# A gated cross-attention and quantised feed-forward block on one core: loads, sums and transposes begin at other places

## What is computed

```python
# x (8, 224, 1024), ctx (8, 750, 1024); Wq, Wk, Wv 1024 x 1024; w1, w2 (2816, 1024), w3 (1024, 2816)
def xattn(x, context):                       # 32 heads of 32
    q = rms(x @ Wq.T); k = rms(context @ Wk.T); v = context @ Wv.T    # rms per head of q and k
    return softmax(q k^T / sqrt(32)) @ v
def ffn(x):                                  # quantise: round(w / mean|w|), clipped to -1..1
    x1 = x @ quantise(w1).T; x2 = x @ quantise(w2).T
    return (sigmoid(x1) * x2) @ quantise(w3).T
x = x + tanh(g_xattn) * xattn(layernorm(x), ctx)
x = x + tanh(g_ffn) * ffn(layernorm(x))
```

## Time and profile before

| | us |
|---|---|
| median of three runs (2461.03 to 2464.95) | 2463.22 |
| the profiled execution, its own time | 2459.92 |
| its span, first to last instruction | 2458.1 |
| PE busy | 2380.9 (97%) |
| DVE busy | 1437.7 (58%) |
| ACT busy | 1351.5 (55%) |
| POOL busy | 856.5 (35%) |
| mean granted clock of TensorE | 0.985 |

### The profile page before, as it was taken

One profiled execution on the slowest core, in us unless ns is written; L12 is line 12 of the kernel. 1 busy time (PEld: TensorE's weight loads), 2 busy tenths in 40 slices (PEclk: granted clock), 3 DMA queues, 4 the chain that ended last, 5 costly groups with the idle time before them and its releaser, 6 DMA issues.

```text
span 2458.1 us, 48877 instructions
## 1 busy us (share of the span) xinstructions
PE 2380.9 (97%) x18386; PEld 1413.2 (57%) x18386; DVE 1437.7 (58%) x2529; ACT 1351.5 (55%) x2886; POOL 856.5 (35%) x857
## 2 busy tenths in 40 slices
PE   7988899999999999999999999878999999999999
PEld 5875466666666666666666666554555555544444
DVE  5656677777776777777767767655444444410000
ACT  5765687787787787887877877752111111110000
POOL 4664245554554645554545546421000000000000
PEclk9998999999999999999999999889999999999999
DMA  6775443343434443433434333444333232344351
GB/s 242 241 242 180 125 102 111 97 119 101 122 93 118 105 107 106 116 116 86 129 102 122 93 93 94 118 122 149 110 95 113 92 114 90 92 137 121 123 163 51
DMA packets 248971, 298.10 MB, mean 121 GB/s; under 512 B 110496, under 2 KB 205216, under 8 KB 248224
## 3 DMA queue, kind: packets, MB, share of 16 engines
q1 hardware_dynamic: 248736, 294.98, 41.3%
HBM read 196.22 MB, written 49.55 MB: 100 GB/s over the span
## 4 chain that ended last, share of the span: by engine, by line
POOL 32%; PE 32%; issue 31%; DMA 2%; DVE 2%; ACT 1%; POOLq 1%; SPq 0%; DVEq 0%; ACTq 0%
PE ps L1435 20%; POOL krs L699 13%; PE ps L1563 11%; POOL oinv L717 4%; POOL qrs L661 3%; POOL kms L694 3%; POOL osum L715 2%; POOL ca L729 2%; POOL osum L722 2%; POOL cn L743 1%; POOL oinv L719 1%; POOL qms L658 1%; DMA hid<-hidden 1%; POOLq L60 1%; PE ps L1420 0%
## 5 line engine op out<-in xcount | busy, mean ns | idle before, releaser
L1467 PE MATMUL ps<-wk,cpair 128*128 128x512 f16 x4608 | 1120.9, 380 | 4.1 <-DVE cpair L1070 3.5
L1267 DVE TENSOR_TENSOR plo<-pf,phi 125x448 f16<-125x448 f32 x768 | 504.6, 658 | 236.1 <-ACT phi L935 229.8
L1467 PEld LDWEIGHTS ps<-wk,cpair 128*128 128x128 f16 x4608 | 400.3, 97 | 379.6 <-issue 6.8
L944 ACT ACTIVATE pf<-ps 125x448 f32<-125x448 f32 x768 | 417.8, 544 | 270.6 <-PE ps L1487 258.6
L1435 PE MATMUL ps<-xnTh,w12q 128*128 128x512 f16 (+1 forms) x1408 | 478.4, 353 | 2.1 <-issue 2.1
L1435 PE MATMUL ps<-xnTl,w12q 128*128 128x512 f16 (+1 forms) x1408 | 478.1, 353 | 0.0
L935 ACT ACTIVATE phi<-pf 125x448 f16<-125x448 f32 x768 | 444.3, 578 | 8.5
L699 POOL TENSOR_TENSOR krs<-kms,mhalf 125x8 f32<-125x8 f32 x192 | 330.0, 1719 | 15.0
L1487 PEld LDWEIGHTS ps<-qT,kst 128*125 128x125 f16 x1536 | 210.1, 138 | 154.2 <-DMA kst<-kpair 7.2
L694 POOL TENSOR_TENSOR kms<-kss,keps 125x8 f32<-125x8 f32 x192 | 69.6, 362 | 625.7 <-DVE kss L1222 625.7
L1511 PE MATMUL ps<-val,phi 125*128 125x65 f16 x3072 | 280.1, 192 | 2.6 <-DVE plo L1267 2.6
(11 more groups left out here) (115 smaller groups left out, 2663.3 us busy)
## 6 DMA issues: line engine op xcount, KB each, us to landing
gbuf<-in_wffn SPq DMA_DIRECT2D x66, 512.0 KB, 4.8
wraw<-in_wffn SPq DMA_DIRECT2D x66, 512.0 KB, 5.7
kst<-kpair SPq DMA_DIRECT2D x128, 250.0 KB, 4.6
cstream<-in_ctx SPq DMA_DIRECT2D x48, 500.0 KB, 4.5
craw<-in_ctx SPq DMA_DIRECT2D x48, 500.0 KB, 6.0
hid<-hidden SPq DMA_DIRECT2D x7, 2816.0 KB, 12.7
hidden<-hh SPq DMA_DIRECT2D x66, 256.0 KB, 2.1
kst<-kpair SPq DMA_DIRECT2D x128, 125.0 KB, 2.5
```

Of the source, the lines that this page charges most:

```text
L944: act.activation(pf[0:KW, e % 6, :], bank(3 + e % 3)[0:KW, 0:2 * S], ACT.Exp, bias=LN128, scale=SCALE).then_inc(p_ready, 1)
L1267: dve.tensor_tensor(plo[0:KW, e % 6, :, :], pf[0:KW, e % 6, :].rearrange("p (t n) -> p t n", t=2), phi[0:KW, e % 6, :, :], ALU.subtract).t ...
L1467: mm = pe.matmul(bank(pt)[:, :], cpair[:, n % RING, a, kc, :], wkp[g][:, w, kc, :], start=(kc == 0 and m == 0), stop=(kc == KC - 1 and m = ...
```

## The change

It does the following, and nothing is computed otherwise:

- Wq is loaded as 16 pieces of 128x512, first the 8 of the left columns, then the 8 of the right; ACT and DVE split them in this order, with `x_norm2(1, 1)` of DVE between the two groups of 8; PE waits piece by piece in both halves of tile 0.
- SP issues the load of x tile n in step n - 3 of phase A rather than n - 2 (tiles 2 and 3 both in step 0).
- `w_squares` of phase A come two at a time, in steps (3, 0), (3, 1), (9, 0), (9, 1).
- The first context tile is split one half-step earlier: ACT after `qnat` of h = 26, DVE at the head of h = 27.
- The 66 absolute sums begin at step 15 of unit 0; steps 11 of units 4 and 5 take one each. SP issues the loads of a unit's sums inside that unit.
- The load of the key/value weights of group 3 moves from unit 0 to unit 1, behind `stack_k`; their squares, sum and splits come later in unit 1, and the power on POOL one tile later.
- The first three `stage` loads are issued in unit 31, and `stage` lies where the dead weights of group 0 were.
- In the tail the transposes use banks 2, 1, 0 in turn, and each waits for the copy three half-tiles back. All 32 matmuls of block 0 come after the tail, and wait for all 28 copies. `thresholds` runs at step 8 instead of 10.

```diff
@@ -127,7 +127,7 @@
         wqraw_scope = ExitStack()
-        wqraw = sb(wqraw_scope, "wqraw", [P, 4, D], F32)
+        wqraw = sb(wqraw_scope, "wqraw", [P, KC, 512], F32)
@@ -182,9 +182,9 @@
         pc = ExitStack()
+        stage = sb(pc, "stage", [LT, 3, 2, D], F16)
         xnTh = sb(pc, "xnTh", [P, KC, TOK], F16)
         xnTl = sb(pc, "xnTl", [P, KC, TOK], F16)
-        stage = sb(pc, "stage", [LT, 3, 2, D], F16)
@@ -205,7 +205,7 @@
         gates_in = sem("gates_in"); tanh_ready = sem("tanh_ready")
-        wq_in = [sem(f"wq_in{i}") for i in range(4)]
+        wq_in = [sem(f"wq_in{i}") for i in range(KC)]
@@ -330,12 +330,12 @@
         def x_bank(h):
-            return 2 + max(h - NX, 0)
+            return (2, 1, 0)[h % 3] if h < NX else 2 + h - NX
 ...
-            wait(eng, xnTd_ready, h - act_halves(h))
+            wait(eng, xnTd_ready, max(h, 0) - act_halves(h))
@@ -355,18 +355,21 @@
         CHUNK_STEPS = (4, 7, 10, 13)
-        W_A_SQUARES = {(2, 0): (0, 0), (2, 1): (0, 1), (3, 0): (0, 2), (3, 1): (0, 3),
-                       (8, 0): (1, 0), (8, 1): (1, 1), (9, 0): (1, 2), (9, 1): (1, 3)}
+        W_A_SQUARES = {(3, 0): (0, 0), (3, 1): (0, 2),
+                       (9, 0): (1, 0), (9, 1): (1, 2)}
 ...
-        W_B_SQUARES = {8: (0, 1), 10: (2, 3)}
-        W_B_SPLIT = {18 + n: 2 * n for n in range(KC // 2)}
+        W_B_SQUARES = {(0, 8): (0, 1), (0, 10): (2, 3), (1, 13): (0, 1), (1, 15): (2, 3)}
+        W_B_SUM = (3, 4)
+        W_B_SPLIT = {(0, 18): (0, 1), (0, 19): (2, 3), (0, 20): (4, 5), (0, 21): (6, 7),
+                     (1, 21): (0, 1, 2), (1, 22): (3, 4, 5), (1, 23): (6, 7)}
 ...
+        GATE_STEPS = sorted([(u, r) for u in range(U) for r in (15, 23)] + [(4, 11), (5, 11)])
@@ -388,10 +391,10 @@
                 sp.dma_start(xraw[:, i, :], x_d[i, :, :]).then_inc(x_in[i], 16)
-            for kc in range(KC):
-                if kc >= 4:
-                    sp.wait_ge(wqlo_ready, kc - 3)
-                sp.dma_start(wqraw[:, kc % 4, :], wq_d[:, kc, :]).then_inc(wq_in[kc % 4], 16)
+            for n in range(2 * KC):
+                wait(sp, wqlo_ready, n - KC + 1)
+                sp.dma_start(wqraw[:, n % KC, :], wq_d[:, n % KC, 512 * (n // KC):512 * (n // KC) + 512]
+                             ).then_inc(wq_in[n % KC], 16)
@@ -421,9 +424,10 @@
                         load_ctx(n)
-                if not last:
-                    sp.wait_ge(xn_ready, i + 1)
-                    sp.dma_start(xraw[:, par, :], x_d[i + 2, :, :]).then_inc(x_in[par], 16)
+                for n in ((2, 3) if i == 0 else (i + 3,)):
+                    if n < NT:
+                        sp.wait_ge(xn_ready, n - 1)
+                        sp.dma_start(xraw[:, n % 2, :], x_d[n, :, :]).then_inc(x_in[n % 2], 16)
@@ -508,10 +512,7 @@
                         load_gates(1)
-                        load_gates(2)
-                        load_gates(3)
                         load_qT(u, par, b, g)
-                        load_w_kv(3)
@@ -526,14 +527,21 @@
                         stack_k(u - 1, 1)
+                        if u == 1:
+                            load_w_kv(3)
 ...
-                        load_gates(2 * u + 2)
-                        load_gates(2 * u + 3)
+                        if u == U - 1:
+                            sp.wait_ge(kv_ready, KT * (U - 3))
+                            for i in range(3):
+                                load_stage(i)
+                        for m, (v, _) in enumerate(GATE_STEPS):
+                            if v == u:
+                                load_gates(m)
@@ -545,8 +553,6 @@
                     sp.wait_ge(kv_ready, KT * U)
-                    for i in range(3):
-                        load_stage(i)
@@ -753,7 +759,7 @@
                         attend_out(u - 2, par, t - 3)
-                    if t == 4 and w_late(u):
+                    if w_late(u) and t == W_B_SUM[u] + 1:
@@ -776,9 +782,10 @@
             x_high(0, 0)
-            for kc in range(KC):
-                act.wait_ge(wq_in[kc % 4], 16 * (kc // 4 + 1))
-                act.activation(wqhi[:, kc, :], wqraw[:, kc % 4, :], ACT.Copy).then_inc(wqhi_ready, 1)
+            for n in range(2 * KC):
+                kc, cols = n % KC, slice(512 * (n // KC), 512 * (n // KC) + 512)
+                act.wait_ge(wq_in[kc], 16 * (n // KC + 1))
+                act.activation(wqhi[:, kc, cols], wqraw[:, kc, :], ACT.Copy).then_inc(wqhi_ready, 1)
@@ -841,14 +848,16 @@
                     if (i, c) in W_A_SQUARES:
-                        w_squares(*W_A_SQUARES[i, c])
+                        gw, m = W_A_SQUARES[i, c]
+                        w_squares(gw, m)
+                        w_squares(gw, m + 1)
 ...
-                    if h == 2 * NT - 1:
+                    half_high(h, c)
+                    if h == 2 * NT - 2:
                         act.wait_ge(csc_ready, 1)
                         ctx_high(0)
-                    half_high(h, c)
@@ -907,11 +916,11 @@
                         act.activation(knat[0:KW, pt, :, 0, :], khat[0:KW, :, :], ACT.Copy).then_inc(khi_ready, 1)
-                    if w_late(u) and r in W_B_SQUARES:
-                        for n in W_B_SQUARES[r]:
+                    if (u, r) in W_B_SQUARES:
+                        for n in W_B_SQUARES[u, r]:
                             w_squares(w_late(u), n)
-                    if w_late(u) and r in W_B_SPLIT:
-                        w_high(w_late(u), range(W_B_SPLIT[r], W_B_SPLIT[r] + 2))
+                    if (u, r) in W_B_SPLIT:
+                        w_high(w_late(u), W_B_SPLIT[u, r])
@@ -1007,11 +1016,13 @@
             x_low(0, 0)
-            for kc in range(KC):
-                dve.wait_ge(wqhi_ready, kc + 1)
-                dve.tensor_tensor(wqlo[:, kc, :], wqraw[:, kc % 4, :], wqhi[:, kc, :].bitcast(F32),
+            for n in range(2 * KC):
+                kc, cols = n % KC, slice(512 * (n // KC), 512 * (n // KC) + 512)
+                if n == KC:
+                    x_norm2(1, 1)
+                dve.wait_ge(wqhi_ready, n + 1)
+                dve.tensor_tensor(wqlo[:, kc, cols], wqraw[:, kc, :], wqhi[:, kc, cols].bitcast(F32),
                                   ALU.subtract).then_inc(wqlo_ready, 1)
-            x_norm2(1, 1)
@@ -1101,6 +1112,8 @@
                     h = 2 * i + c
+                    if h == 2 * NT - 1:
+                        ctx_low(0)
@@ -1122,8 +1135,6 @@
                         ctx_tables(chunk_at(i - 1))
-                    if h == 2 * NT - 1:
-                        ctx_low(0)
@@ -1205,7 +1216,7 @@
                         weight_sums()
-                    if k == U and r == 10:
+                    if k == U and r == 8:
@@ -1248,15 +1259,15 @@
                                         ).then_inc(kpair_ready, 1)
-                    if w_late(u) and r == 14:
+                    if w_late(u) and r == 4 * W_B_SUM[u] + 2:
                         w_norm(w_late(u), bank(2)[:, 256:256 + WQ])
-                    if w_late(u) and r in W_B_SPLIT:
-                        w_low(w_late(u), range(W_B_SPLIT[r], W_B_SPLIT[r] + 2))
+                    if (u, r) in W_B_SPLIT:
+                        w_low(w_late(u), W_B_SPLIT[u, r])
                     if u < G - 1 and r == 22:
                         w_tables(u + 1)
-                    if (r in (15, 23) or (u == 0 and r in (7, 11))) and projects(k):
-
-                        m = {7: 0, 11: 1, 15: 2 * u + 2, 23: 2 * u + 3}[r]
+                    if (u, r) in GATE_STEPS:
+
+                        m = GATE_STEPS.index((u, r))
@@ -1358,7 +1369,7 @@
                     if first:
-                        pe.wait_ge(wqlo_ready, kc + 1)
+                        pe.wait_ge(wqlo_ready, KC * c + kc + 1)
@@ -1397,7 +1408,7 @@
                 for c in range(2):
-                    q_half(2 * i + c, i, par, c, first and c == 0)
+                    q_half(2 * i + c, i, par, c, first)
@@ -1414,8 +1425,15 @@
                     pe.wait_ge(kpair_ready, KT * U)
-                elif h <= NX:
-                    xn_copied(pe, h)
+                if h == 1:
+                    pe.wait_ge(khat_ready, KT * U)
+                    pe.wait_ge(v3_ready, KT * U + 1)
+                if h == 2:
+                    pe.wait_ge(thr_step, 1)
+                if h < NX:
+                    xn_copied(pe, h - 2)
+                if h == NX:
+                    xn_copied(pe, NX)
@@ -1430,7 +1448,7 @@
                     if p < 8:
-                        xn_copied(pe, halves_of(c0, w))
+                        xn_copied(pe, halves_of(c0, w) if p else NX)
@@ -1520,9 +1538,9 @@
                         wait(pe, kpair_ready, T - 2)
-                        if w_late(u) and t == 3:
+                        if w_late(u) and t == W_B_SUM[u]:
                             w_sum(w_late(u), bank(2)[:, 256:256 + WQ])
-                        if w_late(u) and t == 4:
+                        if w_late(u) and t == W_B_SUM[u] + 1:
@@ -1532,16 +1550,13 @@
```

(5 more changed lines are left out.)

## The result

The changed kernel takes 2432.22 us (median of 4 runs, 2427.1 to 2435.5), the kernel before in the same comparison 2462.12: a ratio of 0.9877, with a 95% interval of 0.9863 to 0.9891. The prediction was 2426.2 with 2413 to 2442 as its range. The profiled execution took 2427.1 us with a span of 2425.3, against 2458.1 before. A second comparison with the same kernel, which stands among the experiments, gave 2430.86.

The account below looks back on a forecast made before the run. Bounds: PE's few single waits with clock falls behind them, phase A's chain, and the tail's single bank. Terms sum to -37 from the profiled 2459.9, giving 2422.9; plus 3.3 for the median, 2426.2 us, range 2413 to 2442.

Parts of the forecast that it names:

- the likeliest case: Whole kernel: the sum of the steps holds, 2426 us, own range 2417 to 2435; chance 0.48.
- The sum of -37: Whole kernel: all eight steps added, in us against the profiled execution of 2459.9; negative means faster.
- Wq: -3: Start: column order removes at most PE's 6.3 us of waits for pieces; ends 0 and -6.3, middle taken.
- x tiles and squares: -8: Phase A: earlier x loads end DVE's waits, paired squares cost about 1 us; ends -10.5 and -5.
- First context tile: -0.5: End of phase A: PE's gain on tile 0 is waited for at tile 1; ends -3.5 and +3.
- Sums at 7 and 11: -7.5: Unit 0: PE's 5.8 us wait for knat and about 1.7 of slow clock go; ends -5.8 and -9.
- wkraw behind kst: -8: First scores of unit 1: the 5.5 us kst wait and 2.6 of slow clock go; ends -4 and -9.
- Unit 1: +2: Group 3's squares and splits enter the full softmax pipeline, power about a step late; ends 0 and +6.
- Step 11 of units 4 and 5: +1: DVE waits some 2 us for the sums' block, then sums for 1.2; little reaches PE; ends 0 and +5.
- The tail: -13: Early stage, three banks, 1.55 us a step, block 0 separate: done at 1637.2 against 1649.8; ends -5 and -19.
- The rival "the tail stays at 1.2 GHz": Tail: all steps take 1.72 us, block 0 starts slowly; tail gives -5, total 2434; chance 0.2.
- The list of what would show it: Profile after: knat, kst, wqlo waits at most 1 us, no x waits, unit 1 scores near 250, tail 40 to 45.

Follow-up runs that it names:

- phase_a_undo: Changed kernel with Wq in rows, single sums of squares and the first context tile rounded at h = 27 again, earlier x loads kept; 2431.11 us.
- the four mended kernels: Changed kernel with start loads, unit 1 weights, extra sums and fourth stage load rearranged; three with later feed-forward roundings, one cut in two; 2422.05, 2416.13, 2416.12, 2416.53 us.
- gates_back: Changed kernel with the absolute sums back at steps 7 and 11 of unit 0, none at step 11 of units 4 and 5; 2435.29 us.
- early_wkraw: Changed kernel with group 3's wkraw loaded in unit 0 ahead of the kst copies again, its squares, sum and splits at the old steps; 2437.04 us.
- fixes: Changed kernel with x tiles 2 and 3 loaded earlier, group 3's squares and splits spread, extra sums at step 19, fourth stage tile ahead of feed-forward weights; 2422.05 us.
- one_bank: Changed kernel with one bank for the tail's transposes, block 0 still behind the tail; 2455.72 us.
- old_tail: Changed kernel with one transpose bank and block 0 inside tail steps 20 to 35 again, early stage loads and earlier thresholds kept; 2445.28 us.

## Why the prediction was right, and where its steps failed

Sign and size were right: 2432.2 and 2430.9 measured against 2426.2, inside its own range of the likeliest case. The sum of -37 met -32.8 in the first profile and -28 in the second. That it came so near is in part luck: in the first profile four places ahead of the tail fell 10.7 us short of the forecast (2.1 at the start, 2.5 in phase A, 2.1 in units 4 and 5, and 4.0 in unit 1, where errors of 2.6 and about 5 already stood against each other), while the tail won 5.2 more than forecast and the other places 1.4. By its steps:

- *Wq: -3.* Measured -0.9; phase_a_undo says 1.2. The end at nothing was nearly right, and the reason was in the step: `x_norm(2)` stands ahead of `qhat` on DVE, and its tile lies behind Wq and `wkraw`. DVE waits 3.15 us for it in the changed kernel. The middle was a poor choice, since the row of SP's order already told which end decides; the four mended kernels, which at the start change only this order, win 2.1 to 2.6 us.
- *x tiles and squares: -8.* Measured -5.5 and -6.3, within the ends. To h = 26, without the first context tile, it is -6.5 and -7.3. The step gave the whole 6.7 us of the half-step from 16 to 17 to x. The runs showed two waits of about the same end there, DVE's for x and ACT's for `wkraw`: x alone takes 2.3 us of it, and 5.2 in all of phase A. The later squares, which I had entered only as a cost of 1, cost 2.2 and win 4.2.
- *First context tile: -0.5.* 0 to -0.4, and tile 1 waits as forecast.
- *Sums at 7 and 11: -7.5.* Unit 0 won 7.6 and gates_back lost 9.1; between profiles with the same clock ahead of the wait it is 7.2 and 6.1. Right.
- *wkraw behind kst: -8.* -10.6 us, beyond the end of -9: PE's wait in early_wkraw was 7.3, not 5.5, probably because PE now comes earlier by more than the transfer does.
- *Unit 1: +2.* The step that failed most: 5.7 to 6.3 by fixes, and 6.6 to 7.2 by early_wkraw, the upper end of 0 to +6 or above it. The 2.13 us for the power were foreseen ("about a step too late"). What I left out is that the 2 MB land after step 13 (2.29 us) and that blocks of three splits hold `phi` and `pf` for 1.9 us each; the six buffers of `pf` and `plo` did not cover both.
- *Step 11 of units 4 and 5: +1.* +3.1 and +5.8, less the 0.6 of unit 6. DVE waited 4.8 and 3.6 us instead of some 2, and three steps of `plo` did not cover that.
- *The tail: -13.* -14.3 to -18.2 over the six profiles with this tail, -15.3 in the middle. Parts: the stage loads gave 5; the third `kst` part cost a wait of 3.3 us at step 10 as forecast; a step costs 1.2 us by ACT, and from the third transpose (1576.5) to the last (1609.3) 1.31 on average with its waits, not 1.55: this is the term that was too large, by some 6 us. The rival "the tail stays at 1.2 GHz" is refuted from 1590 on, where the clock is 1.00. The Trainium skill (TensorE: Matmul & The Clock Gate, Part 4: PE-mode transpose) would have had it low; these rows do not agree. In them PE had scores and products between the transposes, so they say nothing of transposes alone; and with one bank the clock was low for 50 us without wide matmuls (one_bank) and 1.00 soon after they joined (old_tail).

The list of what would show it was met except for five: PE waited once 4.1 us for `qhat`, once 3.1 for `wqlo` and once 3.3 for `kst` (in the tail, where another step of the prediction had it), DVE waited for x once at the start, and the transposes took 38 us instead of 40 to 45. The first scores of unit 1 came at 254.2, and no new wait of PE exceeds 3 us in phase B.

## What to carry to other kernels

Before moving a transfer away from a wait, look for the instruction that will need it at its new place and count from the landing, not from the issue: here 10.6 us were won and 7.2 given back 10 us later, and spreading the same work over free steps kept both. Where two transfers end at the same time, expect little from moving one of them: a third of the wait here. Work that costs nothing where it stands, as block 0 in the tail, must not be moved before what makes its place cheap is gone, here the waits for the single bank and the low clock behind them; and a wait taken from one engine brings it sooner to the next one in its queue, as DVE with its roundings.

## What was unexpected of the hardware

- With transposes of 112 columns, scores of 224 and products of 65 and 33 columns and no wide matmul, PE was granted 2.4 GHz for 20 us (1.00 from 1590 to 1610) when it hardly stood between them (at most 0.6 us once the first 1.3 were over). With the same instructions and waits of up to 2.7 us before about half of the transposes (one_bank) it had 0.50 to 0.81 for 50 us. With the same waits and two wide matmuls a step (old_tail) it had 1.00 again, from 1610 on.
- Where the clock falls behind the same waits differs from run to run. Unit 0 takes 33.5 us in five profiles and 35.2 to 36.4 in five others with the same work there (in old_tail the clock is 1.00 from 200 to 210 and 0.66 from 210 to 220, in the changed kernel 0.83 and 1.00), the tail 896.9 and 900.4 us in the same kernel. A gain of 3 us at one place can't be read from one profile of each version.
